# A chain of four layers: the probabilities of two cross attentions transposed in blocks on VectorE instead of on TensorE

## What is computed

```
def _cross_attention(q_in, kv_in, wq, bq, wk, bk, wv, bv, wo, bo, bias_k, bias_v):
    qh = (q_in @ wq + bq).reshape(b, q_len, H, K)        # H = 16 heads of K = 128
    kh = (kv_in @ wk + bk).reshape(b, t, H, K)
    vh = (kv_in @ wv + bv).reshape(b, t, H, K)
    kh = concatenate([kh, bias_k]); vh = concatenate([vh, bias_v])    # one learned row: 376 keys
    logits = einsum('bqhk,bthk->bhqt', qh, kh) / sqrt(K)
    weights = softmax(logits, axis=-1)
    ctx = einsum('bhqt,bthk->bqhk', weights, vh).reshape(b, q_len, H * K)
    return ctx @ wo + bo
```

## Time and profile before

| | us |
|---|---|
| median of three runs (3342.27 to 3354.45) | 3344.55 |
| the profiled execution's own time | 3347.8 |
| its span, first to last instruction | 3346.5 |
| busy: TensorE matmul, share of the span | 3100.5, 93% |
| TensorE weight load | 2582.6, 77% |
| VectorE | 1352.8, 40% |
| ScalarE | 1125.6, 34% |
| GpSimd | 989.1, 30% |
| mean granted TensorE clock | 0.959 |

### The profile page before, as it was taken

How to read it: one execution, slowest core, us unless ns; L and a number is a source line. 1 busy time by engine, 2 the same in 40 slices (tenths; PEclk the granted TensorE clock), 3 DMA queues, 4 the chain that set the end, 5 groups by cost and what they waited for, 6 DMA issues and landing times.

```text
span 3346.5 us, 43816 instructions
## 1 busy us (share of the span) xinstructions
PE 3100.5 (93%) x16648; PEld 2582.6 (77%) x16648; DVE 1352.8 (40%) x3056; ACT 1125.6 (34%) x2508; POOL 989.1 (30%) x922
## 2 busy tenths in 40 slices
PE   5888897999999999999999999999899989979988
PEld 2554565888988888888989888888788777758876
DVE  4784785433332333333333333333211354551133
ACT  3332334433223223332222222233332444443331
POOL 3562563222112122221221221222352232335410
PEclk8897898999999999999999999999899999989989
DMA  5653651333122121122121221111011101101122
GB/s 178 194 176 127 196 172 53 112 127 112 56 78 91 69 87 69 69 87 71 69 100 52 73 98 67 73 69 68 26 64 55 58 24 40 42 28 66 51 93 78
DMA packets 95094, 285.93 MB, mean 85 GB/s; under 512 B 8280, under 2 KB 52824, under 8 KB 86056
## 3 DMA queue, kind: packets, MB, share of 16 engines
q1 hardware_dynamic: 94408, 282.44, 24.7%
q10 hardware_dynamic: 480, 0.69, 0.1%
HBM read 260.94 MB, written 22.15 MB: 85 GB/s over the span
## 4 chain that ended last, share of the span: by engine, by line
PE 73%; DVE 6%; POOL 6%; ACT 5%; DMA 5%; issue 4%; SPq 0%; POOLq 0%; ACTq 0%; DVEq 0%
PE bank L179 21%; PE bank L180 20%; PE bank L181 20%; PE bank L1776 5%; POOL W_lo L219 3%; PE bank L1761 2%; DMA W_raw<-in_weights 2%; DMA v_spread<-v_rows 1%; PE bank L2343 1%; ACT prob L2454 1%; ACT W_hi L210 1%; PE bank L632 1%; DVE prob L2550 1%; DMA att<-in_ctxT 1%; DVE max L1969 1%
## 5 line engine op out<-in xcount | busy, mean ns | idle before, releaser
L2050 POOL TENSOR_SCALAR prob<-prob,inverse 112x376 f32<-112x376 f32 x256 | 143.5, 580 | 1285.5 <-DVE inverse L1975 1285.5
L219 POOL TENSOR_TENSOR W_lo<-W_raw,W_hi 128x1024 fp32r<-128x1024 f32 x138 | 328.6, 2403 | 163.0 <-ACT W_hi L210 160.2
L179 PE MATMUL bank<-ctx_hi,W_hi 128*128 128x376 f32 x1024 | 352.6, 344 | 4.1 <-DVE K_lo L261 2.8
L180 PE MATMUL bank<-ctx_lo,W_hi 128*128 128x376 f32 x1024 | 342.6, 335 | 0.0
L181 PE MATMUL bank<-ctx_hi,W_lo 128*128 128x376 f32 x1024 | 342.0, 334 | 0.0
L261 DVE SCALAR_TENSOR_TENSOR K_lo<-bank,vectors,K_hi 128x375 fp32r<-128x375 f32 (+1 forms) x288 | 172.9, 606 | 413.0 <-ACT K_hi L252 413.0
L179 PE MATMUL bank<-act_hi,W_hi 128*128 128x448 f32 x800 | 319.2, 399 | 11.7 <-DVEq L340 5.6
L180 PE MATMUL bank<-act_lo,W_hi 128*128 128x448 f32 x800 | 298.7, 373 | 0.0
L181 PE MATMUL bank<-act_hi,W_lo 128*128 128x448 f32 x800 | 298.3, 373 | 0.0
L1922 DVE TENSOR_TENSOR V<-bank,bv 128x512 f32<-128x512 f32 x168 | 116.1, 691 | 437.5 <-PE bank L1776 236.4
L1858 ACT ACTIVATE prob<-bank,minus 112x376 f32<-112x376 f32 x256 | 143.4, 573 | 433.5 <-DVE minus L1972 433.5
(11 more groups left out here) (248 smaller groups left out, 6423.4 us busy)
## 6 DMA issues: line engine op xcount, KB each, us to landing
W_raw<-in_weights SPq DMA_DIRECT2D x69, 1024.0 KB, 4.9
ctx_hi<-ctx_split SPq DMA_DIRECT2D x64, 752.0 KB, 4.3
ctx_lo<-ctx_split SPq DMA_DIRECT2D x64, 752.0 KB, 5.9
v_spread<-v_rows SPq DMA_DIRECT2D x128, 224.0 KB
att<-in_ctxT SPq DMA_DIRECT2D x16, 376.0 KB, 4.8
ctx_split<-W_hi SPq DMA_DIRECT2D x16, 376.0 KB, 2.6
ctx_split<-W_lo SPq DMA_DIRECT2D x16, 376.0 KB, 3.6
W_hi<-ctx_split SPq DMA_DIRECT2D x32, 188.0 KB, 4.0
```

Source lines behind the costliest of these rows:

```text
L179: nc.tensor.matmul(dst, left[0], right[0], start=first, stop=False)
L180: nc.tensor.matmul(dst, left[0], right[1], start=False, stop=False)
L219: pool.tensor_tensor(k.Wl[:, slot, cs, :], k.Wraw[:, cs, :], k.Wh[:, slot, cs, :].bitcast(F32), ALU.subtract).then_inc(*k.w_low.now((n, i)))
L2050: pool.tensor_scalar(k.Pm[:, h, :], k.Pm[:, h, :], k.rsum[:, h:h + 1], 1.0, ALU.mult, ALU.mult).then_inc(*k.prob_done.now((n, h)))
```

## The change

In the cross attentions TensorE no longer transposes the probabilities: step "t" is gone from the orders, from the banks and from ScalarE's and VectorE's programs, with `pe_prob_turn`, `act_prob_turned` and the old `dve_prob_turned`. The new `dve_prob_turned` lets VectorE write prob_T from prob directly, SBUF to SBUF: `dve.transpose` turns square blocks of 32 x 32; one instruction takes 32 partitions (block r of the queries) and, for a pair of heads and the three key tiles, 32 columns (block f of the keys), and writes them to the 32 partitions of block f. That is 16 instructions a pair and 32 a unit. Both buffers grow to full blocks (112 to 128 queries, 376 to 384 keys) and prob is set to zero once at the start. VectorE issues eight of the 32 after K_lo of head 1 (n > 0), eight after head 2, and sixteen after head 3. A new semaphore prob_turned counts pairs; the product with V waits for the second pair and the exponentials of the next unit for theirs.

The order changes with it: in units with values V0, V1, pv, V2, xo, late queries, logits; in the first eight units the product comes after the logits and late queries. ScalarE's and VectorE's o_hi and o_lo move accordingly.

```diff
--- before.py
+++ after.py
@@ -1650,22 +1650,20 @@
     steps = [("q", gg, 0, h) for h in range(HK)] if b == 0 else []
     steps += [("K", n, 0)]
     steps += [("xo", n - 2)] if n >= 2 and made(n - 1) else []
-    for h in range(1, HK):
-        steps += [("K", n, h)] + ([("t", n - 1, h - 1)] if n else [])
-    steps += [("t", n - 1, HK - 1)] if n else []
+    steps += [("K", n, h) for h in range(1, HK)]
     steps += [("turn", *turns_of(n))] if turns_of(n) else []
     late = [("q", gg, 1, h) for h in LATE_QUERIES.get(b, ())]
     if made(n):
-        steps += [("L", n, 0), ("L", n, 1)] + ([("pv", n - 1)] if n else []) + [("L", n, 2), ("L", n, 3)] + late
+        steps += [("L", n, h) for h in range(HK)] + late + ([("pv", n - 1)] if n else [])
     else:
-        steps += [("V", n, 0), ("pv", n - 1), ("V", n, 1), ("xo", n - 1), ("V", n, 2)] + late + [("L", n, h) for h in range(HK)]
+        steps += [("V", n, 0), ("V", n, 1), ("pv", n - 1), ("V", n, 2), ("xo", n - 1)] + late + [("L", n, h) for h in range(HK)]
     return steps
 
 def plan_xattn(k):
     u = k.banks
     keys = [s for n in range(len(UNITS)) for s in unit_steps(n) if s[0] != "L"]
     n = len(UNITS)
-    keys += [("t", n - 1, h) for h in range(HK)] + [("turn", 2, B - 2), ("pv", n - 1), ("xo", n - 1), ("turn", 2, B - 1)]
+    keys += [("turn", 2, B - 2), ("pv", n - 1), ("xo", n - 1), ("turn", 2, B - 1)]
     u.rotate(keys, [0, 1, 2, 3], two=("K", "pv", "turn"))
     for n in range(len(UNITS)):
         for h in range(HK):
...
@@ -1752,19 +1751,9 @@
     mm3(k.nc, k.banks.tile(key)[0:T, 0:SP], (k.qh[:, h, :], k.ql[:, h, :]), (k.Kh[:, h, :], k.Kl[:, h, :]), True,
         True).then_inc(*k.banks.filling(key))
 
-def pe_prob_turn(k, n, h):
-    pe, key = k.nc.tensor, ("t", n, h)
-    pe.wait_ge(*k.prob_done[n, h])
-    pe.wait_ge(*k.banks.free(key))
-    bank = k.banks.tile(key)
-    for j, (k0, kn) in enumerate(KTILES):
-        m = pe.transpose(bank[0:kn, j * T:(j + 1) * T], k.Pm[:, h, k0:k0 + kn], k.ident[0:T, 0:T])
-    m.then_inc(*k.banks.filling(key))
-
 def pe_attend(k, n):
     pe, key = k.nc.tensor, ("pv", n)
-    for h in range(HK):
-        pe.wait_ge(*k.banks.drained(("t", n, h)))
+    pe.wait_ge(*k.prob_turned[n, 1])
     if made(n):
         pe.wait_ge(k.vt_loaded, 32 * (n + 1))
     else:
@@ -1773,7 +1762,7 @@
     bank = k.banks.tile(key)
     for h in range(HK):
         for j, (k0, kn) in enumerate(KTILES):
-            m = pe.matmul(bank[:, h * T:(h + 1) * T], k.Vt[0:kn, j, h * P:(h + 1) * P], k.PT[0:kn, h, j, :],
+            m = pe.matmul(bank[:, h * T:(h + 1) * T], k.Vt[0:kn, j, h * P:(h + 1) * P], k.PT[0:kn, h, j, 0:T],
                           start=j == 0, stop=j == 2)
     m.then_inc(*k.banks.filling(key))
 
...
@@ -1845,17 +1830,14 @@
         act.wait_ge(*k.banks.filled(("L", 8 * gg - 1, HK - 1)))
     act.copy(k.Kh[:, :, S], k.vec[:, at:at + HK]).then_inc(*k.learned_high.now(gg))
 
-def act_prob_turned(k, n, h):
-    act, key = k.nc.scalar, ("t", n, h)
-    act.wait_ge(*k.banks.filled(key))
-    act.copy(k.PT[:, h].rearrange("p j t -> p (j t)"), k.banks.tile(key)[:, 0:3 * T]).then_inc(*k.banks.draining(key))
-
 def act_exp(k, n, h):
     act, key = k.nc.scalar, ("L", n, h)
     act.wait_ge(*k.minus_done[n, h])
     if n:
-        act.wait_ge(*k.banks.filled(("t", n - 1, h)))
-    act.activation(k.Pm[:, h, :], k.banks.tile(key)[0:T, 0:SP], ACT.Exp, bias=k.nb[:, h:h + 1], scale=SCALE1,
+        act.wait_ge(*k.prob_turned[n - 1, h // 2])
+    else:
+        act.wait_ge(k.prob_zeroed, 1)
+    act.activation(k.Pm[0:T, h, 0:SP], k.banks.tile(key)[0:T, 0:SP], ACT.Exp, bias=k.nb[:, h:h + 1], scale=SCALE1,
                    accum_out=k.ssum[:, h:h + 1]).then_inc(*k.banks.draining(key))
 
 def act_attended(k, n):
...
@@ -1922,10 +1899,23 @@
     dve.tensor_tensor(k.Vt[0:kn, j, :], k.banks.tile(key)[0:kn, :], k.bv[0:kn, j // 2, :],
                       ALU.add).then_inc(*k.banks.draining(key))
 
-def dve_prob_turned(k, n, h):
-    dve, key = k.nc.vector, ("t", n, h)
-    dve.wait_ge(*k.banks.filled(key))
-    dve.tensor_copy(k.PT[:, h].rearrange("p j t -> p (j t)"), k.banks.tile(key)[:, 0:3 * T]).then_inc(*k.banks.draining(key))
+
+BLOCK = 32
+
+def dve_prob_turned(k, n, pair, blocks):
+
+    dve, hs = k.nc.vector, slice(2 * pair, 2 * pair + 2)
+    if blocks[0] == 0:
+        dve.wait_ge(*k.prob_done[n, 2 * pair + 1])
+        if n:
+            dve.wait_ge(*k.banks.filled(("pv", n - 1)))
+    for f in blocks:
+        for r in range(P // BLOCK):
+            rows = k.Pm[BLOCK * r:BLOCK * r + BLOCK, hs, :].rearrange("p h (j s) -> p h j s", j=3)
+            m = dve.transpose(k.PT[BLOCK * f:BLOCK * f + BLOCK, hs, :, BLOCK * r:BLOCK * r + BLOCK],
+                              rows[:, :, :, BLOCK * f:BLOCK * f + BLOCK])
+    if blocks[-1] == P // BLOCK - 1:
+        m.then_inc(*k.prob_turned.now((n, pair)))
 
 def dve_attended(k, n):
     dve, key, bank = k.nc.vector, ("pv", n), k.banks.tile(("pv", n))
@@ -1975,6 +1965,7 @@
         dve.reciprocal(k.rsum[:, h:h + 1], k.ssum[:, h:h + 1]).then_inc(*k.inverse_done.now((n, h)))
 
 def dve_xattn(k):
+    k.nc.vector.memset(k.Pm[:], 0.0).then_inc(k.prob_zeroed, 1)
     for n, (gg, b) in enumerate(UNITS):
         turn = turns_of(n)
         for h in range(HK):
@@ -1985,27 +1976,26 @@
                 dve_output(k, n - 2)
             if turn and h == 1:
                 dve_norm_in(k, *turn)
-            if n and h == 1:
-                dve_prob_turned(k, n - 1, 0)
+            if n and h:
+                dve_prob_turned(k, n - 1, 1 if h == 3 else 0, (2, 3) if h == 2 else (0, 1))
             if turn and h == 2:
                 dve_norm_out(k, *turn)
         if n:
-            dve_prob_turned(k, n - 1, 2)
+            dve_prob_turned(k, n - 1, 1, (2, 3))
         if turn:
             dve_low_turned(k, ("turn", *turn), turn[1])
-        if made(n):
-            if n:
-                dve_attended(k, n - 1)
-        else:
+        if not made(n):
             dve_values(k, n, 0)
+            dve_values(k, n, 1)
             dve_attended(k, n - 1)
-            dve_values(k, n, 1)
+            dve_values(k, n, 2)
             dve_output(k, n - 1)
-            dve_values(k, n, 2)
         dve_logits(k, n)
+        if n and made(n):
+            dve_attended(k, n - 1)
     n = len(UNITS) - 1
-    dve_prob_turned(k, n, 0)
-    dve_prob_turned(k, n, 2)
+    for pair in range(2):
+        dve_prob_turned(k, n, pair, (0, 1, 2, 3))
     dve_norm_in(k, 2, B - 2)
     dve_norm_out(k, 2, B - 2)
     dve_low_turned(k, ("turn", 2, B - 2), B - 2)
@@ -2047,7 +2037,7 @@
             pool_next_norm(k, *turns_of(n))
         for h in range(HK):
             pool.wait_ge(*k.inverse_done[n, h])
-            pool.tensor_scalar(k.Pm[:, h, :], k.Pm[:, h, :], k.rsum[:, h:h + 1], 1.0, ALU.mult,
+            pool.tensor_scalar(k.Pm[0:T, h, 0:SP], k.Pm[0:T, h, 0:SP], k.rsum[:, h:h + 1], 1.0, ALU.mult,
                                ALU.mult).then_inc(*k.prob_done.now((n, h)))
         for w in splits_last(n):
             pool_split_weight(k, w)
@@ -2987,7 +2977,7 @@
     k.qh, k.ql = sb("q_hi", [P, HK, T], F32R), sb("q_lo", [P, HK, T], F32R)
     k.oh, k.ol = sb("o_hi", [P, HK, T], F32R), sb("o_lo", [P, HK, T], F32R)
     k.Kh, k.Kl = sb("K_hi", [P, HK, SP], F32R), sb("K_lo", [P, HK, SP], F32R)
-    k.Vt, k.Pm, k.PT = sb("V", [P, 3, D]), sb("prob", [T, HK, SP]), sb("prob_T", [P, HK, 3, T])
+    k.Vt, k.Pm, k.PT = sb("V", [P, 3, D]), sb("prob", [P, HK, 3 * P]), sb("prob_T", [P, HK, 3, P])
     k.bv = sb("bv", [P, 2, D])
     k.mxs, k.nb, k.ssum, k.rsum = (sb(n, [T, HK]) for n in ("max1", "minus1", "sum1", "inverse1"))
```

More of the change, by code:

```diff
@@ L1681, in plan_xattn @@
         s.expect(units)
+    k.prob_turned.expect([(n, pair) for n in range(len(UNITS)) for pair in range(2)])
     for s in (k.qs_high, k.qs_low):
@@ L1800, in pe_xattn @@
                 pe_keys(k, *which)
-            elif what == "t":
-                pe_prob_turn(k, *which)
             elif what == "turn":
@@ L1813, in pe_xattn @@
     n = len(UNITS) - 1
-    for h in range(HK):
-        pe_prob_turn(k, n, h)
     pe_next_turn(k, 2, B - 2)
@@ L1884, in act_xattn @@
             act_high(k, key, k.Kh[:, h, 0:S], k.banks.tile(key)[:, 0:S], V(k, f"bk{gg // G + 1}", gg % G * HK + h))
-            if n and h == 2:
-                act_prob_turned(k, n - 1, 1)
-        if n:
-            act_prob_turned(k, n - 1, 3)
         if turns_of(n):
@@ L1891, in act_xattn @@
             act_turned(k, ("turn", layer, i), i, NEXT_NORM[layer] + "_s", NEXT_NORM[layer] + "_o")
-        if n:
+        if not made(n):
             act_attended(k, n - 1)
-        if not made(n):
             for h in LATE_QUERIES.get(b, ()):
@@ L1901, in act_xattn @@
                 act_queries(k, gg, 1, h)
+            if n:
+                act_attended(k, n - 1)
         for w in splits_last(n):
@@ L1904, in act_xattn @@
     n = len(UNITS) - 1
-    act_prob_turned(k, n, 1)
-    act_prob_turned(k, n, 3)
```

(1 more changed line is left out.)

## The result

The changed kernel takes 3782.1 us (median of four, 3775.15 to 3785.01) where the kernel before, on the same chip, takes 3346.02: ratio 1.1296, 95% interval 1.1269 to 1.1323. The sum gave 3627 and the range ended at 3725, so the sign was right and the size was short by 155 us.

What follows compares the result with a forecast made beforehand. TensorE was taken to bound the kernel, so only its work and new waits count. Stalls +193, first eight units +32, stage's end +7 and clock +50 made +282 us on the earlier kernel: 3627 us, range 3395 to 3725.

Steps and rivals of the forecast that it cites:

- The rival that the transposes overlap: VectorE's transposes overlap, one starting every 0.27 us, with no clock loss counted: 3407 us; chance 0.20.
- T: Time from the start of one VectorE block transpose to the next; taken as 0.354 us, without overlap.
- 1792T: Transpose time in seven groups of eight units with values; 1792T - 432 - 9 gave the added time.
- The stall's formula: In plain units the last transpose ends 6.53 + 32T us after the keys' start, and TensorE's product with V waits for it.
- 32T - 7.33: TensorE's stall before the product with V in a plain unit, in us; forecast 4.0.
- 193: Added us over seven groups of eight units with values, stalls less saved TensorE transposes and waits, at T = 0.354.
- The clock: Slower TensorE work after stalls of 5.1 us and over: 25 stalls at 2 us each, +50 us.
- Made units: First eight units, whose values are made before: product waits for the transposes; 131.9 us before, 162.7 after, together +32 us.
- Units with a row turned: Units turning a normalised row: VectorE's norm comes between, but costs the old order about the same wait; nothing added.
- The end: Stage's end: the last unit's transposes stand free between the last reciprocal and the norm; +7 us, at least +5.2.
- Costed at nothing: Probabilities' memset, VectorE's values, low part and output after the product, the moved output, and the saved VectorE and ScalarE copies: 0 us.
- the sum's 81 for TensorE: Gain from taking the transposes off TensorE: 72 us over 64 units, plus about 9 us of waits.

Runs made afterwards that it cites:

- the run with one head at a time: The changed kernel with each VectorE transpose cut in two, one head each (64 of 96 elements a unit): 3877.25 us in one execution.
- run with twenty fills: The changed kernel with 20 identity matmuls added before TensorE's wait for the turned probabilities (or for the normalised row, where one is turned): 3675.88 us, ratio 1.0979.
- the run of the order: The kernel before the change with only its order of steps changed, transposes and copies left as they were: 3345.13 us, ratio 0.9993.
- four heads at a time: The changed kernel with one transpose for all four heads (32 x 384), so 16 a unit instead of 32: 3584.0 us, ratio 1.0702.

## Why the prediction was wrong in size

**Direction and mechanism: right.** The rival that the transposes overlap (T = 0.27) fell: T is 0.382. The reason given, that each reads another block of partitions than its predecessor, is what the run with one head at a time shows. The Trainium skill ("VectorE: DVE Perf Modes", section "Two Vector instructions with no wait between them") has it as a rule, and the trace agrees with it: 202 ns from start to start where the block is kept, 239 where it changes.

**T: 0.354 forecast, 0.382 measured.** The length is 369 ns, 15 more than the sum of a one-element instruction and 192 x 1.10 ns, and the next one starts 13 ns after the end, which I hadn't counted. The formula 1792T turns that 0.028 into 50 us, and the made units' seven times 32T into 6. The same page of the Trainium skill gives, in its section on the trn2 errata, 58 cycles of overhead in the table and about 150 in the text below it; I quoted the table. With 150 cycles at its 0.96 GHz the estimate is (192 + 150) / 0.96 = 356 ns, close to the measured 369; the 0.26 of the table is not.

**The stall's formula: right.** 6.53 + 32T with T = 0.382 gives 18.75 us for the product's start; it is 18.9, and 20.5 for b = 1 and 5 (20.35). The stall of 4.93 answers to 32T - 7.33 = 4.89. Since the formula holds, 193 should have been 243.

**The clock: the step that failed.** The sum took a loss of 2 us for 25 stalls of 5.1 us and more, 50 us, and none for the 4 us stalls of the plain units. The only row that I had showed a stall of 5.13 us with a slow product behind it; none showed that one of 4 us is free, and I treated it as if one did. With the measured T even the plain stalls reach 4.9. The product is slow behind 4.9 us, behind 3.7, and in part behind 2.1. The price per stall is larger as well, up to 2.5 us in the product and 0.4 in the values behind: in the plain unit shown the granted clock stays at the lower of its levels (1.2 and 2.4 GHz) through the whole product. Where a row is turned, the stall stands ahead of the row, and the slow work is the row's and the values': two tiles of values take 6.7 to 7.9 us instead of 5.6, and the product behind them its 2.60 again, with the same buffers and data. The run with twenty fills puts at least 106 us on this term, where the sum had 50.

**Made units: +54.6 for +32.** 6 us are T. TensorE stands idle 48.8 us in the seven (3.6 before): 21.5 ahead of the product, as forecast in kind; 20.6 ahead of the last head's logits, 2.9 in each, which is the line on K_lo in the table of waits; and 6.7 ahead of the output step, for o_lo. The forecast had put K_lo of head 3 behind sixteen transposes, but only as time of VectorE; that TensorE's logits wait for it is a step it left out. In all but unit 3 the product still waits for the transposes afterwards, so that this wait costs TensorE no time of its own; but the clock is low behind it (the late query step of unit 2 takes 4.7 us for 2.4). The work without idle time takes 148.7 us, and 129.0 in the run with thirty left out, whose order is the same: about 20 us at the lower clock, where the clock's 50 us had counted 8. Four products there last 4.6 to 5.0 us, 9 of these 20. The place of the product alone costs nothing, as the run of the order shows.

**Units with a row turned: right for a wrong reason.** "It costs the old order about the same wait, so I add nothing": the wait is 83.8 us in the 14 units, and was 4.6 in four of them. The half of the transposes that precedes the norm was overlooked. It doesn't show in the sum, since the run with the norm moved forward only shifts the wait; these 13 units become 4.9 to 6.4 us longer, about as the plain ones (5.8 to 7.0).

**The end: +7 forecast, about +9 measured.** The transposes stand free there, 12.26 us of them, and the last product takes 5.33 us at the lower clock, 4.25 before.

```profile
2806.88 12.26 DVE L1915 STREAM_TRANSPOSE prob_T<-prob 32x192 f32<-32x192 f32 x32
```
```profile
2821.61 1.01 PE L228 MATMUL bank<-ident,normalised 112*128 112x112 f32 x4 [17.86 <-DVE normalised L1951]
2822.41 5.33 PE L1765 MATMUL bank<-prob_T,V 128*128 128x112 f32 x24
```

**Costed at nothing: right.** The order moved nothing (3345.13 us). No run takes out VectorE's and ScalarE's saved copies alone, but the 76 us gained with thirty transposes left out are no more than the sum's 81 for TensorE, so nothing is left for them.

The account of the 433 us inside the stage: 232 of the sum without the clock, 57 for T, 102 shown for the clock by the fills; 42 are left. 17 of them lie in the made units (54.6 for 32 + 6), which the fills didn't mend, and 16 in the products that stay slow behind fills with b = 1 and 5 (44.7 us for eleven instead of 28.6). Some 9 stay without a number. So of the 155 us by which the sum fell short, T has 57, and the clock at least 52. The range had allowed for a T of 0.38, up to 3720 us; it is the clock that took the time beyond it.

## What to carry to other kernels

Work moved off the busiest engine has to fit the time in which nothing waits for it: here TensorE gave up 1.1 us a unit and VectorE needed 12.2, of which only 7.3 were free. Sum it for each kind of unit: the tightest kind loses first, and with the work divided between the engines 13 units took back nearly all that 42 had gained. And cost a stall of TensorE at more than its length: the work behind 4.9 us of standing still took up to 2.9 us longer at half the clock, and a stall of a length that the trace doesn't show is not free because it is shorter than one that it shows.

## What was not expected of the hardware

- A stall of 2.1 us lowered the clock behind it in some plain units and not in others (product of 2.7 to 4.3 us with four heads at a time).
- The block transpose costs 169 ns an instruction and 1.04 ns an element: 369 ns for 192, 569 for 384. At 96 elements the durations alternate, 267 and 226 ns, with the overlap.
- TensorE works faster with work added: twenty identity matmuls in each stall, whose results nothing uses, took the kernel from 3782 to 3676 us.
